# A tower of recurrence, banded attention and experts: the second bias scaled by the gate on ScalarE and added on GpSimd, with a new order of steps

## What is computed

```python
z, f, o = tanh(conv(x, Wz)), sigmoid(conv(x, Wf)), sigmoid(conv(x, Wo))   # conv over 2 neighbouring rows
c = f * c + (1 - f) * z ; h = o * c                                       # recurrence along the rows
h = h + attention(layernorm(h))      # 8 heads, 39 fixed offsets back (0..32, 48, 64, 96, 128, 192, 256), gated
# experts: top 2 of 64, each expert takes 128 rows in all, one shared pair of matrices
y = gelu(buf @ w1.T + b1) @ w2.T + b2
gate = where(keep, p, 0) ; h = h + sum over the kept picks of y * gate
```

## Time and profile before

| | before |
|---|---|
| device time, median of 3 runs | 443.13 us (442.23 to 443.18) |
| the profiled execution | 445.57 us, span 443.8 us |
| PE busy | 416.6 us, 94% of the span |
| DVE busy | 384.3 us, 87% |
| POOL busy | 372.8 us, 84% |
| ACT busy | 324.2 us, 73% |

### The profile page before, as it was taken

How to read it: one execution, slowest core, us unless ns; L and a number is a source line. 1 busy time by engine, 2 the same in 40 slices (tenths; PEclk the granted TensorE clock), 3 DMA queues, 4 the chain that set the end, 5 groups by cost and what they waited for, 6 DMA issues and landing times.

```text
span 443.8 us, 12681 instructions
## 1 busy us (share of the span) xinstructions
PE 416.6 (94%) x4554; PEld 284.5 (64%) x4554; DVE 384.3 (87%) x873; ACT 324.2 (73%) x728; POOL 372.8 (84%) x389
## 2 busy tenths in 40 slices
PE   8768888999999999999999999999999999998884
PEld 5333545576767767676767767676767675757663
DVE  2247899999999999999999999999999999997562
ACT  3355776968788696868788797868788787867773
POOL 7529799999998989899898989899898999995611
PEclk9869999999999999999999999999999999999888
DMA  8303366372644627272644627272734546465200
GB/s 288 120 0 102 83 193 167 111 192 62 151 136 119 177 65 199 78 193 67 155 128 114 180 73 209 63 192 68 171 110 114 162 108 169 108 169 133 93 18 17
DMA packets 78702, 56.08 MB, mean 126 GB/s; under 512 B 28304, under 2 KB 71344, under 8 KB 78512
## 3 DMA queue, kind: packets, MB, share of 16 engines
q1 hardware_dynamic: 78640, 55.28, 45.9%
HBM read 35.56 MB, written 19.70 MB: 125 GB/s over the span
## 4 chain that ended last, share of the span: by engine, by line
PE 71%; DVE 6%; POOL 6%; issue 4%; ACT 2%; POOLq 0%; DVEq 0%; ACTq 0%
PE bank L417 18%; PE bank L506 8%; PE bank L483 8%; PE bank L393 5%; PE bank L367 5%; PE bank L445 5%; PE bank L368 4%; PE bank L433 4%; PE bank L425 3%; POOL fprod L1173 2%; DVE prod L886 2%; PE bank L475 2%; POOL prod L1188 2%; PE bank L401 2%; PE bank L385 2%
## 5 line engine op out<-in xcount | busy, mean ns | idle before, releaser
L1188 POOL TENSOR_TENSOR prod<-q,k 128x1496 f32<-128x1496 f32 x48 | 144.5, 3027 | 29.1 <-ACT k L653 15.8
L886 DVE SCALAR_TENSOR_TENSOR prod<-bank,par,k 128x1496 f32<-128x1496 f32 x80 | 141.0, 1765 | 5.1 <-ACT q L647 5.1
L417 PE MATMUL bank<-prod,ew 128*32 128x374 f32 x1024 | 87.7, 479 | 2.9 <-POOL prod L1188 1.8
L1173 POOL TENSOR_TENSOR fprod<-q,k 128x374 f32<-128x374 f32 (+6 forms) x112 | 80.1, 749 | 0.0
L417 PEld LDWEIGHTS bank<-prod,ew 128*32 128x32 f32 x1024 | 31.2, 109 | 47.7 <-issue 38.6
L754 ACT ACTIVATE hid<-bank,par 128x374 f32<-128x374 f32 x64 | 36.7, 574 | 27.2 <-PE bank L483 25.1
L587 ACT ACT_TABLE_LOAD x40 | 51.3, 1283 | 1.5 <-PEq L1322 0.7
L483 PE MATMUL bank<-x,par 128*128 128x374 f32 x128 | 49.3, 496 | 0.7 <-ACT x L707 0.7
L506 PE MATMUL bank<-par,hid 128*128 128x128 f32 x384 | 47.9, 276 | 0.3 <-ACT hid L754 0.3
L506 PEld LDWEIGHTS bank<-par,hid 128*128 128x128 f32 x384 | 45.9, 192 | 2.9 <-issue 0.4
L367 PE MATMUL bank<-xT,par 128*128 128x374 f32 x96 | 42.8, 529 | 2.7 <-DMA xT<-x_dram 2.6
(11 more groups left out here) (119 smaller groups left out, 877.7 us busy)
## 6 DMA issues: line engine op xcount, KB each, us to landing
band<-band_scratch SPq DMA_DIRECT2D x16, 768.0 KB, 4.9
band_scratch<-attn SPq DMA_DIRECT2D x64, 180.4 KB, 3.0
vnear<-v_scratch SPq DMA_DIRECT2D x48, 192.0 KB, 2.9
v<-v_scratch SPq DMA_DIRECT2D x32, 192.0 KB, 4.1
v_scratch<-vtok SPq DMA_DIRECT2D x16, 192.0 KB, 2.8
xT<-x_dram SPq DMA_DIRECT2D x16, 187.5 KB, 3.3
vfar<-v_scratch SPq DMA_DIRECT2D x16, 128.0 KB, 3.3
out_dram<-osb SPq DMA_DIRECT2D x16, 128.0 KB
```

What stands on the lines that cost most here:

```text
L417: done = mm(home(f"s{c}")[32 * g:32 * g + 32, lo:N], ew[:, c * CW + j, :], src[:, j, lo:N], start=first or only, stop=last or only)
L886: v.scalar_tensor_tensor(bass.AP(prod[c][:, :, :].tensor, part * N, [[CW * N, 128], [PARTS * N, w], [1, N]]), home("q")[:, 0:N].unsqueeze( ...
L1173: last = g.tensor_tensor(fprod[:, i, o:N], q[q_.s][:, o:N], k[q_.s][:, KPAD:KPAD + N - o], ALU.mult)
L1188: g.tensor_tensor(bass.AP(prod[c][:, :, :].tensor, part * N, [[CW * N, 128], [PARTS * N, w], [1, N]]), q[q_.s][:, :].unsqueeze(1).broadcas ...
```

## The change

b2 is no longer added to the sum in PSUM by DVE. ACT scales b2 by gt into a new buffer extra (scale_b2, three instructions of 128x128), POOL adds h2 to it (add_extra, 128x384), and finish adds extra instead of h2. All lists of steps are written in another order, HOME is dealt out anew, and the pipeline has one turn more: down for a sequence stands in the turn after its logits.

```diff
@@ scalar @@
+            def scale_b2(q_):
+                act.wait_ge(gt_ready, q_.b + 1)
+                after(act, out_ready, q_.b - 1)
+                for t in range(TT):
+                    done = A(extra[q_.s][:, t, :], P("b2"), ACT.Identity, bias=zeroc[:, 0:1], scale=gt[:, t:t + 1])
+                done.then_inc(scaled_ready, 1)
@@ vector @@
-            def add_b2(q_):
-                dve.wait_ge(down_mm, TT * (q_.b + 1))
-                rows = home("dn")[:, 0:TT * D].rearrange("p (t d) -> p t d", d=D)
-                v.tensor_tensor(rows, rows, P("b2").unsqueeze(1).broadcast_to([128, TT, D]), ALU.add).then_inc(y1_ready, 1)
             def finish(q_):
-                dve.wait_ge(y1_ready, q_.b + 1)
-                dve.wait_ge(gt_ready, q_.b + 1)
+                dve.wait_ge(down_mm, TT * (q_.b + 1))
+                dve.wait_ge(extra_ready, q_.b + 1)
...
-                                                  h2[q_.s][:, t, :], ALU.mult, ALU.add)
+                                                  extra[q_.s][:, t, :], ALU.mult, ALU.add)
@@ gpsimd @@
+            def add_extra(q_):
+                pool.wait_ge(scaled_ready, q_.b + 1)
+                g.tensor_tensor(extra[q_.s][:, :, :], extra[q_.s][:, :, :], h2[q_.s][:, :, :], ALU.add).then_inc(extra_ready, 1)
@@ tensor, turn (of the new list, shortened) @@
+                    score(a4, 1, 1, ("up0", a7), ("g", a4), first=True)
+                    score(a4, 1, 3)
+                    score(a4, 1, 2)
+                    score(a4, 0, 3)
+                    score(a4, 1, 0, last=True)
+                    score(a4, 2, 0, ("op", a6), ("dn", a8), ("s2", a5), first=True)
+                    score(a4, 0, 1, last=True)
+                    score(a4, 2, 1, last=True)
...
+                    down(a7, 2, ("s2", a4), ("op", a6), ("dn", a8), head=True)
...
+                    down(a7, 0)
...
+                    down(a7, 1)
...
+                    out_project(a5, ("dn", a7), ("s2", a4))
...
+                    up(a6, 0, ("g", a3), ("pv", a5), ("k", a3), ("xb", a3), ("s1", a4), ("up0", a7))
...
                     turn_h(a2, ("ht", a3))
...
+                    positions(a6, ("o", a1), ("ts2", a4), ("pos", a7))
+                if a3:
+                    score(a3, 0, 0, ("up2", a6), ("ot", a5), ("lg", a6), ("tb1", a5), ("s0", a4), first=True)
                     score(a3, 0, 2)
-            pipeline(pe, turn, range(BATCH + 6))
+            pipeline(pe, turn, range(BATCH + 7))
@@ gpsimd, turn @@
+                if a5:
+                    far_sum(a5, 3)
+                    carry(a5)
+                    far_sum(a5, 4)
+                    far_sum(a5, 5)
+                if a7:
+                    add_extra(a7)
+                if a3:
+                    local_products(a3, 2, head=True)
...
+                    far_products(a3, 0)
+                    far_products(a3, 1)
                 if a6:
                     kept_mask(a6)
                     kept_weights(a6)
+                if a4:
+                    far_sum(a4, 1)
...
```

More of the change, by code:

```diff
@@ L141, in build @@
         hid = sb("hid", [128, FC, NP])
+        extra = [sb(f"extra{s}", [128, TT, D]) for s in range(2)]
         osb = [sb(f"osb{s}", [128, TT, D]) for s in range(2)]
@@ L534, in turn @@
                     attend(a5, 2)
-                    attend(a5, 1)
+                    attend(a5, 0)
+                if a3:
+                    value_project(a3, ("tb2", a5), ("ts0", a4), ("f", a1))
+                if a6:
+                    up(a6, 1, ("tb0", a5), ("x2b", a6))
+                if a7:
+                    down(a7, 0)
+                if a5:
+                    turn_o(a5, ("lg", a6), ("tb1", a5))
+                if a7:
+                    down(a7, 1)
+                if a3:
+                    project(a3, "g", ("pv", a5), ("k", a3))
@@ L776, in turn @@
                     softmax_far(a4)
+                    softmax_exp(a4)
+                if a5:
+                    open_gate(a5)
+                if a3:
+                    value_rows(a3)
+                if a6:
+                    router_exp(a6)
+                    gelu(a6, 1)
+                if a3:
+                    tanh_gate(a3)
                 if a1:
@@ L1100, in turn @@
                 if a3:
-                    products(a3, 0, 3)
+                    products(a3, 0, 1)
+                if a0:
+                    recur_in(a0)
                 if a6:
+                    take_room(a6)
                     gate_sum(a6)
-                    add_b2(a6)
+                if a0:
+                    recur(a0)
+                if a6:
                     gate_weight(a6)
@@ L1114, in turn @@
                     score_add(a3, 0)
+                    score_add(a3, 2)
+                    score_max(a3)
+                if a4:
+                    softmax_rcp(a4)
+                if a3:
+                    score_subtract(a3)
+                if a2:
+                    products(a2, 0, 2, head=True)
+                if a5:
+                    route_max(a5)
+                    route_picks(a5)
+                if a4:
+                    attention_sum(a4)
+                if a5:
+                    route_mask(a5)
+                if a4:
+                    attention_norm(a4)
+                if a3:
+                    near_values(a3)
+                if a4:
+                    attention_gate(a4)
+                if a2:
+                    products(a2, 1, 0)
+                if a6:
+                    finish(a6)
+                if a2:
+                    products(a2, 0, 0)
+                if a4:
+                    residual(a4)
+                if a0:
+                    recur_out(a0)
+                if a4:
+                    stats2(a4)
             pipeline(dve, turn, range(BATCH + 6))
```

247 lines of the change are left out of this document (87 added, 160 removed).

## The result

The changed kernel takes 452.33 us (median of 4 runs, 451.65 to 452.68) against 443.15 (442.23 to 444.24): 1.0208 times as long, 95% interval 1.0185 to 1.0231. I had forecast 446.0, with 449.0 as the upper end. The direction was right and the size was not. The profiled execution of the changed kernel took 452.38 us, like its median.

The account below looks back on a forecast made before the run. PE's own work was taken to bound the middle, unchanged; a 2.7 to 2.8 us lead from filling is lost in the emptying, and the end with half clock makes plus 2.85: 443.13 + 2.85 = 446.0, range 441.3 to 449.0.

Parts of the forecast that it names:

- The bound and the middle: Nine middle turns: only PE's own work counts, 24.87 us each again, within 0.05; the edit is worth nothing there.
- rival C: Middle: 0.25 us of air before score (0,3) is missing, DVE and PE wait each turn; 447.6 to 449.3, chance 0.15.
- two-sides rule: GpSimd and two-SBUF-input VectorE instructions exclude each other; taken as nothing, at worst 1.0 us a turn, nearly hidden.
- Filling: Turns 3 to 5: POOL sets the pace, turn_x stays at 84.0; the middle then starts 2.7 us earlier.
- the whole 2.7 us of downs: Last filling turn, PE-bound: three downs of 0.89 us not yet there, so the middle starts 2.7 us earlier, work owed.
- The three short turns: Emptying up to the last scores: 23.45, 21.8 and 21.3 us, 66.5 against 66.7; last scores 2.8 us earlier.
- Emptying, to the rows of b15: From last scores to turn_x2 of b15: from 2.8 us ahead to 0.8 behind, 3.6 lost.
- The wait of gate_sum for kw: Emptying: kw of b12 comes behind the last far products, delaying DVE; band of b15 1.0 us earlier, not 2.8.
- the dip: Granted clock of 0.50 behind PE's idle stretch near turn_x2 of b15, costing 1.65 us, taken in full.
- The last 15 us: Behind turn_x2 of b15: downs of b14 and the bias chain make plus 1.2 in all, plus 2.85 with half clock.
- From the profiled execution to the median: Profiled execution lies 2.44 us above the median; 448.4 on its scale becomes 446.0 on the median's.
- A: Faster: the 2.8 us lead survives to turn_x2; 442.0, or 440.3 if early exponentials help; chance 0.2.

Follow-up runs that it names:

- e3: Changed kernel, in turn 4 alone convolution o of b3 moved behind z and f of b4; 451.26 us, ratio 1.0165.
- e8: Changed kernel with e3, e4, e6 and e7 in one; 446.65 us, ratio 1.0094.
- e4: Changed kernel with three buffers for hkeep in place of two; 451.49 us, ratio 1.017.
- e10: e8 with read_values of b15 issued ahead of its read_band; 448.73 us, ratio 1.0122.
- e9: Changed kernel with five filler matmuls, result overwritten, in each idle stretch of PE ahead of turn_x2 of b14 and b15; 448.38 us, ratio 1.0112.
- e12: Kernel before with five unread matmuls in its idle stretches at the end; 442.6 us over 10 runs, ratio 0.997.
- e16: e12 plus nine unread matmuls in the waits of the start; 440.02 us, ratio 0.993.
- e2: Changed kernel with add_b2 back on DVE ahead of finish, without scale_b2 and add_extra; 455.39 us, ratio 1.026.
- e7: Changed kernel with the downs of b13 and b14 together ahead of turn_x2 of b14 and b15; 447.28 us, ratio 1.0108.
- e1: Kernel before with the bias edit and no more of the new order than it needs; 463.63 us, ratio 1.0424.
- e13: e10 with most of POOL's far work of b15 ahead of kept and kw of b13, carry of b15 behind its last far sum; 446.0 us, ratio 1.0063.
- e15: e13 with the old bias: add_b2 on DVE ahead of finish, no scale_b2 or add_extra; 444.91 us, ratio 1.0046.
- e11: e10 with kept and kw of b12 ahead of the last far products and weights of b15 ahead of scale_b2; 448.55 us, ratio 1.0124.
- e6: Changed kernel, last turns: down 2 behind attend, up 0 ahead of out_project, scale_b2 behind the band copies; 452.61 us, ratio 1.0219.

## Why the prediction was wrong

**The bound and the middle: right.** 24.87 forecast, 24.81 measured. No product made PE wait in the middle, so rival C did not happen. The two-sides rule of the Trainium skill (SBUF — State Buffer, SBUF: two separate sides) that I had weighed took nothing here: with a microsecond more of POOL in each turn, the middle turn grew no longer.

**Filling, the first step that failed.** I wrote that the turns up to turn_x of b3 are paced by POOL and left them at 84.0, 58.67 behind turn_x of b0. It was 59.47. The wait for near_values is 1.31 us in the kernel before and stood nowhere in my sum. In the new order it is 3.50 and the half clock comes on top; mended (e3, e8) turn_x of b3 stands at 58.5. Then I took the whole 2.7 us of downs off the next turn, as if PE alone bound it. It became 1.8 shorter (23.06 for 24.87), in the changed kernel and in e3 and e8 alike, and PE waits 0.65 of the difference for DVE ahead of turn_o. So the lead at b4 was 1.0, and 2.0 with the first wait mended. It grew by 0.6 up to b13, to 1.6, because the nine middle turns are 0.06 shorter each, which I had only as a tolerance of 0.5. The 2.6 of e8 at b13 is near my 2.7 in part by that luck.

**The three short turns: a term missing and a term right.** I counted DVE's work and overlooked keep_rows, which stands between residual and turn_h. The forecast was 23.45, 21.8 and 21.3, measured were 23.15, 23.12 and 21.64; with a third buffer (e4) the first two are 22.93 and 22.55, so 0.8 of the 1.4 us is keep_rows and 0.6 is DVE's order. The lead at the last scores was 0.2 in place of 2.8. These two steps make 2.6 of the 3.3 us by which the chain from turn_x of b0 to the last finish came out longer than forecast (6.17 in place of 2.85).

**Emptying, to the rows of b15: right size, partly wrong cause.** Forecast 3.6 us lost, measured 4.3. The wait of gate_sum for kw that I named had no chance to show, as the scores themselves came late; in e8 it was there, 0.80. The floor at which I put turn_o of b15, 395.7, is where e8 and e10 have it, in e10 by POOL's queue as I wrote; in e8 attend ends 0.1 us behind POOL's far sums. But the changed kernel missed it by 3.3: turn_x2 of b14 is followed by half clock, down 2 and scale_b2 stand ahead of attend, and attend stalled by 1.34. There POOL's far sums were over at 420.5, and DVE's attention_sum waited for attend until 423.4. I had looked for the dip only behind b15.

**The last 15 us: right.** Forecast 2.05 lost there, measured 13.91 against 11.85, 2.06, with scale_b2, add_extra and finish in a row. That both agree to 0.01 is luck: at full clock (e9) the stretch takes 12.56 us where my sum has 12.25, and the half clock then costs 1.35 and not 1.65. In e9, e12 and e16 the idle stretches are filled, and from 411 to 435 us the granted clock stays at 1.00. Unfilled, PE's idle stretches of 3.57 to 3.79 us ahead of turn_x2 came with half clock in nine of ten cases, within them or up to 1 us behind. The tenth is in e2, where the clock stayed at 1.00 for 8 us behind the stretch:

```profile
417.00 0.52 PE L470 MATMUL bank<-par,xrow 128*128 128x128 f32 x3 [3.79 <-ACT xrow L708]
412.00:425.00 13.00, 6.82 (x141) 5.92 (x141) 5.62 (x26) 8.59 (x20) 8.43 (x12) 1.00 0.40 107
```

So the rule on the clock gate that I had cited (the Trainium skill, TensorE: Matmul & The Clock Gate, Part 1: The HAM clock gate) held in these nine cases and does not tell every one.

**From the profiled execution to the median: a step I had not counted as one.** I took 2.44 us off, as if the changed kernel's runs would lie as far under a sum made from an execution of low clock. They did not. The kernel before was profiled at a mean granted clock of 0.977. In the four sessions of the experiments it ran 52 times, at 0.977 to 0.992 with a median of 0.986, in 441.2 to 446.4 us; over these runs 0.01 less clock goes with 2.1 us more, so by my estimate 1.9 of the 2.44 us are the clock. The changed kernel had 0.970 to 0.977 in all four. Short idle stretches of PE are followed by half clock in some executions and not in others: 0.97 and 0.67 us were, in the profile before, where 0.81 and 1.45 us were not, in e8; 1.97 us were in e7 and not in e8. Those of 3.5 us ahead of the convolution o of b3 were in all seven profiles that have them, those of 3.6 to 3.8 in nine of ten. That this explains the 2.4 is argued from the clocks alone. In the profiled run turn_x of b0 also came 0.6 later (25.93 against 25.34), with 6.8 us of half clock ahead of it in place of 4.6. The sum is then 3.3 + 0.6 + 2.4 = 6.3, the distance from 446.0 to 452.3.

**The rivals.** A, faster, had the lead survive up to turn_x2; there was no lead. The price of the edit by itself I had put at 1.7 at the end, nothing elsewhere. It was three different numbers in three orders: 17 to 19 us in the old one (e1), 2 to 3 gained in the new one (against e2, with intervals that just overlap), 1.1 lost in the mended one (e13 against e15, within the noise). I had no term for what it delays behind it.

## What to carry to other kernels

An order that leaves PE idle for microseconds mostly paid twice here, for the wait and for the half clock behind it, so look for idle stretches that precede dense work on the chain and put owed work there, or else matmuls that nobody reads. When banks or buffers are dealt out anew, follow for each reader not only the middle but the first turns and the last: what waits for the bank that this reader holds. And ask of the profiled execution how its clock compares with that of the other runs before the sum is moved to the median.

## What was not expected of the hardware

In the 96 small matmuls of attend and right behind them PE stalls at times for what the profile puts down to no engine: 1.34 us in the changed kernel, 1.90 in e2, 1.02 in e4, 0.81 in e1, at b15; 0.53 in e3 and e9, 0.56 in e11, 0.80 in e7 and 0.83 in e13, all five in the same middle turn and ahead of the same record, the 95th of 96; and 1.27 in e6 in the down that stands behind attend of b15. The middle turn with a stall takes 25.6 to 25.9 us in place of 24.81. The kernel before shows none, and e10 none above 0.2.

The traces point at the instructions. All ten stalls end 1.2 to 1.5 us behind the end of a packet of the instruction queue q8 (in the changed kernel 423.05 and 421.73), though such packets start 6 to 16 us apart. It has 36 of them in the changed kernel (packets, MB, share of the DMA engines):

```profile
q8 instruction: 36, 0.59, 0.6%
```

No run moved those packets, so that PE waits for its instructions there is argued and not shown.

Waits ahead of attend are another matter, though the profile puts them down to no engine either: 1.45 us in e8, 0.75 in e9, 0.68 in e7, 0.49 in e2, all at b15. Each ends 0.09 us behind the landing of the second transfer of read_values, and in e10 this transfer is issued earlier and the wait is gone.

Fourteen unread matmuls, 9 us of PE's work in a kernel of 443, made it 3.4 us shorter (443.47 to 440.02, medians of one session).
